# Diffusion attention: values for two groups at once, sums turned a step later, a norm on VectorE, weights a stage ahead; gated outputs by chunk, fills in another batch

## What is computed

```python
# gated feed-forward, at the end of each of two layers
h = (h - mu) / jnp.sqrt(var + 1e-05) * lg + lb
h = h @ w1 + b1
a, g = jnp.split(h, 2, axis=-1)
h = a * jax.nn.gelu(g, approximate=False)
x = x + h @ w2 + b2

# diffusion attention
def _token_diffusion(x, Wqk, Wv, Wo, tau):
    b, n, d = x.shape
    dh = d // H
    qk = (x @ Wqk).reshape(b, n, H, dh).transpose(0, 2, 1, 3)
    v = (x @ Wv).reshape(b, n, H, dh).transpose(0, 2, 1, 3)
    dot = jnp.einsum('bhnd,bhmd->bhnm', qk, qk)
    q2 = jnp.sum(qk * qk, axis=-1)
    logits = (2.0 * dot - q2[..., :, None] - q2[..., None, :]) / math.sqrt(dh)
    logits = logits * tau
    attn = jax.nn.softmax(logits, axis=-1)
    out = jnp.einsum('bhnm,bhmd->bhnd', attn, v)
    out = out.transpose(0, 2, 1, 3).reshape(b, n, d)
    return out @ Wo
...
x = x + _token_diffusion(_layernorm(x, ln1_w, ln1_b), Wqk_t, Wv_t, Wo_t, tau_t) * gamma1
x = x + _channel_diffusion(_layernorm(x, ln2_w, ln2_b), Wqk_c, Wv_c, Wo_c, tau_c) * gamma2
```

## Time and profile before

| | us |
|---|---|
| median of 3 runs | 4335.49 (4331.86 to 4339.73) |
| the profiled execution | 4336.2 |
| its span | 4334.3 |
| PE busy in the span | 3696.7 (85%) |
| DVE busy | 2398.3 (55%) |
| ACT busy | 1753.8 (40%) |
| POOL busy | 1620.6 (37%) |

### The profile page before, as it was taken

One profiled execution on the slowest core, in us unless ns is written; L12 is line 12 of the kernel. 1 busy time (PEld: TensorE's weight loads), 2 busy tenths in 40 slices (PEclk: granted clock), 3 DMA queues, 4 the chain that ended last, 5 costly groups with the idle time before them and its releaser, 6 DMA issues. The chain is left out here.

```text
span 4334.3 us, 60457 instructions
## 1 busy us (share of the span) xinstructions
PE 3696.7 (85%) x17584; PEld 2203.4 (51%) x17584; DVE 2398.3 (55%) x6529; ACT 1753.8 (40%) x4010; POOL 1620.6 (37%) x1750
## 2 busy tenths in 40 slices
PE   6999999999699998997999899679999998559940
PEld 3565665556355555554555555335555554446630
DVE  6676777767465552225565433245665565355556
ACT  2544555445255553113555511035555555114420
POOL 2343333443566661005666512411222222352244
PEclk8999999999899999999999999779999999669975
DMA  6565666555210113441111211132222221259952
GB/s 104 70 79 71 79 91 86 81 70 70 68 33 34 40 42 111 179 185 57 49 34 39 75 49 61 39 80 58 59 55 55 55 56 42 91 175 318 314 162 70
DMA packets 230322, 377.79 MB, mean 87 GB/s; under 512 B 39822, under 2 KB 166098, under 8 KB 223698
## 3 DMA queue, kind: packets, MB, share of 16 engines
q1 hardware_dynamic: 216658, 355.13, 34.8%
q0 software_dynamic: 6144, 16.79, 1.2%
q10 hardware_dynamic: 7296, 3.22, 0.3%
HBM read 170.03 MB, written 84.93 MB: 59 GB/s over the span
## 5 line engine op out<-in xcount | busy, mean ns | idle before, releaser
L758 DVE CUSTOM_DVE_ANT_0 a_ps<-a_ps,a_mask 128x128 f32<-128x128 f32 (+3 forms) x1024 | 479.7, 512 | 194.2 <-PE a_ps L513 175.6
L2618 DVE TENSOR_REDUCE c_neg_max<-c_ps 128x1 f32<-128x512 f32 x512 | 341.1, 684 | 238.9 <-PE c_ps L2286 237.5
L2479 ACT ACTIVATE c_probsT<-c_ps 128x512 f32<-128x512 f32 x512 | 299.3, 598 | 387.9 <-PE c_ps L2298 379.3
L368 POOL TENSOR_SCALAR_AFFINE_SELECT a_probs_c<-a_probs_c 128x256 f32<-128x256 f32 (+1 forms) x384 | 187.5, 504 | 664.1 <-ACT a_probs_c L663 663.5
L663 ACT ACTIVATE a_probs_c<-a_ps 128x512 f32<-128x512 f32 x640 | 344.9, 602 | 100.1 <-PE a_ps L531 70.4
L513 PE MATMUL a_ps<-a_packed_qk 65*128 65x128 f32 (+3 forms) x1024 | 338.5, 374 | 47.5 <-DVE a_maxima L758 27.4
L1094 POOL TENSOR_TENSOR w_probs<-w_probs,w_inv 128x1024 f32<-128x1024 f32 x128 | 242.3, 1893 | 334.6 <-DVE w_inv L1457 334.6
L549 PE MATMUL a_ps<-a_probs_c,a_v 128*64 128x512 f32 (+3 forms) x2048 | 315.4, 451 | 1.0 <-POOL a_probs_c L368 0.8
L531 PE MATMUL a_ps<-a_packed_qk 67*128 67x512 f32 (+3 forms) x1024 | 288.2, 344 | 1.6 <-DMA a_packed_qk<-a_max_half 1.6
L2286 PE MATMUL c_ps<-c_packed_qk 68*128 68x512 f32 x512 | 260.9, 514 | 4.8 <-DVE c_neg_max L2618 2.5
L1349 ACT ACTIVATE w_probs<-w_ps_s,w_neg_max 128x256 f32<-128x256 f32 x512 | 236.3, 479 | 66.5 <-DVE w_neg_max L1452 65.8
(11 more groups left out here) (323 smaller groups left out, 7743.5 us busy)
## 6 DMA issues: line engine op xcount, KB each, us to landing
a_packed_qk<-a_halves SPq DMA_DIRECT2D x512, 128.0 KB, 4.6
d_w<-in_L_ffn_second SPq DMA_DIRECT2D x71, 516.0 KB, 5.0
d_w<-in_L_ffn_first SPq DMA_DIRECT2D x71, 512.0 KB, 5.1
rows_dram<-f_zeros SPq DMA_DIRECT2D x8, 4096.0 KB, 15.9
c_packed_qk<-c_halves SPq DMA_DIRECT2D x256, 128.0 KB, 2.4
w_v<-w_v_next SPq DMA_DIRECT2D x16, 1024.0 KB, 4.6
d_rows<-rows_dram SPq DMA_DIRECT2D x71, 128.0 KB, 4.3
mixed_dram<-d_y SPq DMA_DIRECT2D x71, 128.0 KB, 5.0
```

Source lines behind the costliest of these rows:

```text
L758: last = nc.vector.tensor_tensor_reduce(tile, tile, mask[:, (NT - 1 - i) * P:], 1.0, -3e38, ALU.add, ALU.max, accum_out=maxima_of[:, hd // ...
L2479: nc.scalar.activation(probsT[:, q % 2, r, :], ps_again[u % 2][:, :], ACT.Exp).then_inc(exp_done.sem, 1)
L2618: nc.vector.tensor_reduce(neg_max[:, g % 2, 0, s % GS:s % GS + 1], bank("s", s)[:, :], AX.X, ALU.max, negate=True).then_inc(max_ready.sem, 1)
```

## The change

1. gated_ffn on POOL: the root of the next batch comes ahead of the fill, and the fill is called in batch 5 (`b + 3 == B`), after a wait for that root.
2. gated_ffn on PE: y is made chunk by chunk, for all four blocks of tokens each, with a wait for each gated chunk in place of one for all.
3. diffusion attention: `project_v` makes two groups (128 columns) in a call, in two calls instead of four. The second half is made at step 26 of its own batch, the first half of the next batch at step 60; ACT brings each over in one copy of 512 columns.
4. Four turned sums stand a step later on PE (9, 25, 41, 57 become 10, 26, 42, 58) and so does their division on DVE; q3 goes from step 6 to 7 on PE and a step later on ACT and DVE.
5. The second norm (`hn2`) moves from POOL to DVE (kind g in `AFTER_MAX`, step 34); POOL makes only its root.
6. The 12 `rest` transfers move from ACT's queue at the stage start to SP's in `ahead_sync`, with their tiles made a stage ahead.
7. The drain: POOL makes the root, then the next stage's `ahead_gpsimd`, then its own output norm; DVE calls `ahead_vector` after step 36 of the drain instead of at its end.

```diff
@@ gated_ffn, POOL and PE @@
-                if b + 2 == B:
+                if b + 1 < B:
+                    roots_in.step(pool, b + 1, 0, rstd[:, :], mv[:, :, 1], EPS, neg_half[:, :])
+                if b + 3 == B:
                     if LAST:
                         pool.wait_ge(y_ready.sem, y_ready.at(b - 1, 1))
+                    pool.wait_ge(roots_in.ready.sem, roots_in.ready.at(b + 1, 1))
                     following.ahead_fill(pool)
-                if b + 1 < B:
-                    roots_in.step(pool, b + 1, 0, rstd[:, :], mv[:, :, 1], EPS, neg_half[:, :])
...
-                pe.wait_ge(gated_ready.sem, gated_ready.at(b, CK))
                 if b >= 1:
                     pe.wait_ge(y_taken.sem, y_taken.at(b - 1, 1))
-                for t in range(NT):
-                    for c in range(CK):
-                        m = part(c)
+                for c in range(CK):
+                    m = part(c)
+                    pe.wait_ge(gated_ready.sem, gated_ready.at(b, c + 1))
+                    for t in range(NT):
                         last = nc.tensor.matmul(ps_y[:, t, :], gated[0:m, c, t * P:(t + 1) * P], w2[0:m, c, :],
-                                                start=c == 0, stop=c == CK - 1)
+                                                start=c == 0 and t % 2 == 0, stop=c == CK - 1 and t % 2 == 1)
@@ diffusion attention, EXTRA @@
-    EXTRA = {0: [("m", 3, -1)], 2: [("q", 2, 0)], 6: [("q", 3, 0)], 9: [("t", 2, -1)], 11: [("v", 2, 0)],
...
+    EXTRA = {0: [("m", 3, -1)], 2: [("q", 2, 0)], 7: [("q", 3, 0)], 10: [("t", 2, -1)], 12: [("n", 1, 0)],
...
@@ ahead_sync @@
         with nc.allow_non_contiguous_dma(reason="a few small vectors, once"):
             for dst, src in first:
                 sp.dma_start(dst, src).then_inc(first_in.sem, 16)
+            for dst, src in rest:
+                sp.dma_start(dst, src).then_inc(rest_in.sem, 16)
@@ POOL @@
-            def norm_between(b):
+            def root_between(b):
                 roots.step(pool, b, 0, rstd[:, :], mv[:, :, 1], EPS, neg_half[:, :])
                 standing_wait(pool, roots.ready.sem, roots.ready.at(b, 1), passed_pool.sem)
-                for t in range(NT):
-                    last = nc.gpsimd.tensor_scalar(hn2[:, t, :], h[:, t, :], mv[:, t, 0:1], rstd[:, t:t + 1],
-                                                   ALU.subtract, ALU.mult)
-                last.then_inc(hn2_ready.sem, 1)
...
             def drain(b):
-                body(b, (-1,))
+                make_h(b - 1)
+                root_between(b - 1)
                 following.ahead_gpsimd(pool)
+                norm_output(b - 1)
@@ PE, project_v @@
-            def project_v(b, j):
-                if j == 0:
+            def project_v(b, f):
+                if f == 0:
                     pe.wait_ge(rest_in.sem, 16 * len(rest))
-                cols = slice(HG * DH * j, HG * DH * (j + 1))
                 for t in range(NT):
                     for k in range(KD):
-                        last = nc.tensor.matmul(bank("v", j)[:, t * HG * DH:(t + 1) * HG * DH],
-                                                hT[:, k, t * P:(t + 1) * P], wv[:, k, cols], start=k == 0, stop=k == KD - 1)
+                        last = nc.tensor.matmul(bank("v", f)[:, t * P:(t + 1) * P], hT[:, k, t * P:(t + 1) * P],
+                                                wv[:, k, f * P:(f + 1) * P], start=k == 0, stop=k == KD - 1)
@@ ACT @@
-            with nc.allow_non_contiguous_dma(reason="a few small vectors, once"):
-                for dst, src in rest:
-                    act.dma_start(dst, src).then_inc(rest_in.sem, 16)
@@ DVE @@
+            def norm_between(b, prior):
+                roots.wait(dve, b, 0)
+                if prior:
+                    dve.wait_ge(hT2_psum.sem, hT2_psum.at(ref(b, -1), KD))
+                for t in range(NT):
+                    last = normalise(nc, hn2[:, t, :], h[:, t, :], mv, rstd, t)
+                last.then_inc(hn2_ready.sem, 1)
...
             def drain(b):
-                body(b, (-1,))
-                following.ahead_vector(dve)
+                for s in range(STEPS):
+                    step(b, s, (-1,))
+                    if s == GS * G // 2 + GS // 4:
+                        following.ahead_vector(dve)
```

More of the change, by code:

```diff
@@ L1906, in diffusion_attention @@
     first.append((neg_norm[:, :, :], con["neg_norm"]))
+    rest = []
+    for dst, src in ((wv, w["Wv_t"]), (wo, w["Wo_t"]), (wqc, w["Wqk_c"]), (wvc, w["Wv_c"]), (woc, w["Wo_c"])):
+        rest.append((dst[:, :, :], src.rearrange("(k p) n -> p k n", p=P)))
+    for n in (1, 2):
+        rest.append((gamma[:, n - 1, :], w[f"gamma{n}"].partition_broadcast(P)))
+    per_group = w["tau_c"].rearrange("(j r) a c -> r (j a c)", r=HG)
+    for r in range(HG):
+        rest.append((tau_c[CDH * r:CDH * r + CDH, :], per_group[r].partition_broadcast(CDH)))
+    rest.append((block_mask[:, :], con["block_mask"]))
     def ahead_sync(sp):
@@ L2709, in extras @@
                         sum_stats(at, n, 1, z_added)
+                    elif kind == "g":
+                        norm_between(at, prior)
                     elif kind == "r":
```

57 lines of the change are left out of this document (25 added, 32 removed), and 18 rows, old and new, of tables (AFTER_EXP, EXTRA).

## The result

The changed kernel takes 4228.94 us, median of 4 runs (4227.27 to 4238.53); the kernel before, run beside it, 4337.61 (4331.86 to 4341.48). The ratio is 0.9744, with a 95% interval of 0.9726 to 0.9761: 109 us less. The forecast was 4253, so the direction held, and so did four of the six terms (the fill, the weights, the loop and the clock). The time lies in the wide range (4224 to 4288), which was made wide for rivals that did not happen. It lies outside the forecast's own range (4236 to 4270): the gain is 26 us larger than the sum of 82.5.

What follows compares the result with a forecast made beforehand. It took PE's own work plus small waits as the bound (740.56 of 805 us busy in the diffusion attention loop). 13.6 + 1.4 + 4.5 + 45 + 12 + 6 = 82.5 gave 4253; range 4236 to 4270, with rivals 4224 to 4288.

Steps and rivals of the forecast that it cites:

- the fill: Last gated_ffn layer: POOL's root goes before its memsets, but the norm in batch 5 is blocked; 1.4 us, bounds −1.2 to 18.4.
- the weights: Start of diffusion attention: 12 transfers issued by SP a stage earlier leave ACT free, hT earlier; 4.5 us, bounds 3.5 to 5.5.
- the loop: Diffusion attention's batches: fewer v calls and shorter PE waits, 5.8 us a batch, 45 in all, bounds 27 to 62.
- the clock: Diffusion attention loop: half-clock stretches behind longer PE stops cost 24 us, half of it regained; 12 us, bounds 0 to 24.
- y by chunk: Both gated_ffn layers: PE's wait before the y matmuls goes, matmul and weight-load counts stay; 13.6 us, bounds 11 to 13.6.
- Rival one: Last gated_ffn layer: the memsets are hidden in batch 5's POOL idle time, 17 us more gain, 4236; chance 0.14.
- Steps 7 to 12: Diffusion attention batch: q3 and sums later and v2 gone; 2.6 us a batch, bounds 1.5 to 4.3.
- the sums' steps: Diffusion attention, steps 24 to 28, and sums at 58 with a wider v: 0.7 us a batch each.
- Steps 33 to 40: Diffusion attention batch: hn on DVE removes PE's wait but delays the maxima; 0.8 us a batch, bounds 0 to 2.1.
- The drain: End of diffusion attention: last hn on DVE 3.6 us, earlier hand-over to mixture 2.4; 6.0 together, bounds 2 to 7.
- New waits: Rival in diffusion attention: waits return elsewhere, the clock still falls, only v calls' matmul time is saved; 4284, chance 0.17.
- all waits and the clock: Rival in diffusion attention: all waits go, 4.3 instead of 2.6, and clock stays up, 24 instead of 12; 4229, chance 0.08.

## Why the prediction was right, and where it was not

- **y by chunk** (13.6 forecast) is the term that was mis-sized. Its waits went as said. What was missed is in the sentence "the count of matmuls and weight loads stays": the count did, the duration of the group didn't. The order alone is worth 18.9 us of busy time (1.2 us a batch in 16 batches), and with the freed waits the first layer gives 19.1 us by itself. The earlier trace rows had 12.00 us for 48 products, 0.250 each; a look at the group by shape, in which the 42-row products stand at 428 ns against 397, would have hinted that something happens where the size changes: one change costs 0.20 us, and the new order saves six of seven a batch. That is 19 of the 26 us; most of the others stand in the same two stages, which gave 39.9 us where 15.0 were forecast. The exact split is rough: in the two runs that take parts out of the changed loop, the first layer has the same code and takes 262.9 and 264.9 us, not 261.45.
- **The fill** (1.4 forecast) was right in its mechanism, and in its size as far as it can be read: the stop is 1.1 us shorter, and the last layer gave 1.7 us more than the first, whose own time varies by 3. The norm took 16.65 us beside the memsets (13.7 + 1.4 and up to 1 more were forecast), PE's stop is 14.34 (13 to 14 forecast), and the start of the kernel was the right row to go by. The 18.01 there is no rate: it is the time until three memsets in a row had ended (6.92, 7.06 and 3.54 us), and in batch 5 it was two. The stop on PE is shorter than the norm, because PE was still busy for 2.4 us of it. Rival one is out as a forecast and right as a plan: the 17 us priced for a hidden fill are 17.05 when the fill is really put behind the norm.
- **Weights a stage ahead**: 4.5 forecast, 4.6 measured.
- **The loop and the clock** (45 + 12 = 57) came to 53.1. In the periods it is 7.2 us a batch: 2.5 of PE's own work, 3.2 of idle time and 1.5 of the clock's 3.1. The forecast of 5.8 a batch without the clock was met by 5.7, by another split: the v calls by themselves are worth the 3.4 forecast (3.5), but 1.0 of it came back as work, and the waits gave 3.2 instead of 2.4. The sentence that failed is that falls stand behind stops of 1.6 us and more: in the changed kernel the clock falls at 3196 behind a stop of 0.68, and in the run with the later sums behind 0.67. The kernel before already had one that did not fit, behind 1.06 in the first batch. Half of the clock's loss, taken as the value between two ends, happened to be right: that is luck.
- **Steps 7 to 12 and the sums' steps** (2.6 + 0.7 + 0.7 of the 5.8) hold the moved steps together with v calls, and price the steps as if their worth did not hang on the rest. By themselves they made the kernel 0.24% slower. As a part of the whole they give 1.4 to 2.5 us a batch.
- **Steps 33 to 40**: a new wait of about 1.0 for maxima was forecast; the waits for maxima are 6.6 us in 9, 0.7 each and 1.2 at most. The norm alone gives 2.3 a batch with its share of the clock, against 0.8 plus the clock's term.
- **The drain**: 3.6 forecast for the norm, 3.6 measured (9.31 less 5.69); 2.4 for the hand-over, 1.6 measured (6.8 less 5.2). Another 2.4 came between; the run with the order of y alone, which has the old code here, took 56.89 where the kernel before took 59.96, so these 2.4 are no more than two profiles of one code can differ by. Neither the drain nor the weights a stage ahead has a run of its own: both rest on the marks of the two profiles.
- **Rivals.** New waits did not take the loop's gain (4284); all waits and the clock did not come back either (4229 would have been the time, by luck almost the one measured, through y instead). VectorE's queue did not stop at step 34.
- **The range.** The terms' bounds, added as independent errors as the prediction says, give about 27 us to the fast side (17 for the fill, 17 for the loop, 12 for the clock) and 22 to the slow side (18 for the loop, 12 for the clock, 4 for the drain): 4226 to 4275, not 4236 to 4270. The measured time lies inside by that sum, but through y, whose bounds allowed nothing.
- **What the profile would show.** Of the signs of being right all came in kind; two are a little off in size: the loop is 752 us (805 less 53; 745 to 750 forecast), and its clock 0.96 (0.97 forecast).
- **Open.** The mixture stage is 2.4 us shorter and the second window attention 1.1, without a change in their code; the profiles of one kernel differ by more than that, so no cause is claimed.

## What to carry to other kernels

When an edit changes the order of matmuls and not their number, read the group by shape before pricing it at nothing: where products of different contraction sizes alternate, each change can cost time (0.20 us here), and sorting them by size cost nothing here. A large memset on GpSimd is only hidden if no VectorE instruction of the excluding form falls into it; look for such an instruction behind the same semaphore that starts the memset, and let the memset wait for it. A stop that is removed is worth its length only if the clock stays where it was, so price idle time and low-clock time as two terms and test the parts apart: here one part alone saved idle time and made the kernel 0.24% slower.

## What the runs showed that was not expected

- Each change between 128-row and 42-row products, in either direction, costs 0.20 us (y takes 12.00 us with seven changes a batch, 11.41 with four, 10.82 with one).
- A VectorE tensor_scalar from SBUF to SBUF waits until the GpSimd memset under way has ended, even for 16 columns: 6.37 us instead of 0.18. A tensor_tensor beside the same memsets does not wait.
- The granted clock fell to the lower level behind stops of 0.67 us, after PE had been busy for 3.67 and 3.33 us of the two stretches of 4 us before, and the fall came in the same place in every batch: all six periods of that run are 105.71 to 105.83. In the changed kernel the periods come in two sizes, 95.94 to 95.99 without a fall and 99.10 to 99.15 with one.
